# Mamba layer on one core: z*C of two groups in eight is added into a neighbouring group by GpSimd-issued accumulating transfers, and TensorE sums six groups

## What is computed

```python
dA  = exp(einsum('bld,dn->bldn', delta, A))          # 512 channels d, 16 states n
dBx = einsum('bld,bln->bldn', delta * x, Bm)
def step(z, inp):
    dA_t, dBx_t, c_t = inp
    z = dA_t * z + dBx_t
    y = einsum('bdn,bn->bd', z, c_t)                 # the sum over the 16 states
    return (z, y)
y = y + x * D
```

## Time and profile before

| what | us |
|---|---|
| median of 3 runs | 3613.94 |
| lowest, highest | 3609.24, 3613.96 |
| the profiled execution's own time | 3609.97 |
| its span, first to last instruction | 3608.1 |
| of it, Mamba phase, about | 50 to 1680 |
| of it, attention phase, about | 1680 to 3608 |

### The profile page before, as it was taken

The page is one execution under the profiler, slowest core; times in us unless marked ns, Lnnn a source line. Parts: engine busy times, 40 slices in busy tenths (PEclk is TensorE's granted clock), DMA queues, the critical chain, the costliest instruction groups (busy, mean ns, idle before and its releaser), DMA issues.

```text
span 3608.1 us, 119462 instructions
## 1 busy us (share of the span) xinstructions
PE 3386.7 (94%) x51938; PEld 1549.7 (43%) x51938; DVE 3122.9 (87%) x3007; ACT 2536.4 (70%) x3847; POOL 1740.1 (48%) x1559
## 2 busy tenths in 40 slices
PE   7999999999999999997899999999999999999997
PEld 4556555555555555554323323233232332332322
DVE  6898888889898888986897997989979989799896
ACT  4666657676666757664398695985958959679598
POOL 5798888879788888975210312203112131121210
PEclk8999999999999999999999999999999999999999
DMA  4544545444544545542702506106052070330700
GB/s 126 140 121 118 142 110 149 124 137 126 141 133 115 147 115 137 138 131 83 119 14 34 85 2 92 28 19 100 2 78 41 3 109 10 60 59 2 106 2 13
DMA packets 145230, 307.74 MB, mean 85 GB/s; under 512 B 24484, under 2 KB 64068, under 8 KB 144452
## 3 DMA queue, kind: packets, MB, share of 16 engines
q1 hardware_dynamic: 144708, 300.10, 36.3%
HBM read 230.68 MB, written 35.13 MB: 74 GB/s over the span
## 4 chain that ended last, share of the span: by engine, by line
PE 18%; ACT 12%; issue 11%; DVE 10%; DMA 1%; SPq 0%; ACTq 0%; DVEq 0%; POOL 0%
ACT probs L1544 12%; PE ps L1331 6%; PE ps L1316 4%; DVE neg_max L1658 2%; PE ps L1433 2%; PE ps L1366 2%; PE ps L1346 1%; PE ps L1378 1%; PE ps L1277 1%; DVE acc L1815 1%; DVE att L1717 1%; DVE acc L1803 1%; DVE x1T L1640 1%; DVE acc L1748 1%; DVE x1T L1638 1%
## 5 line engine op out<-in xcount | busy, mean ns | idle before, releaser
L353 POOL TENSOR_TENSOR z<-z,c_rep 128x1024 f32<-128x1024 f32 x512 | 1369.5, 2686 | 279.5 <-DVE z L878 270.7
L1544 ACT ACTIVATE probs<-ps,e_scale 128x512 f32<-128x512 f32 x2048 | 1242.4, 702 | 116.4 <-PE ps L1316 114.1
L878 DVE TENSOR_TENSOR_SCAN z<-dA,ps 128x1024 f32<-128x1024 f32 x512 | 1158.8, 2279 | 164.8 <-PE ps L411 114.9
L1658 DVE TENSOR_REDUCE neg_max<-ps 128x1 f32<-128x1024 f32 x1024 | 1187.8, 1217 | 43.9 <-PE ps L1277 42.3
L725 ACT ACTIVATE dA<-rep,a_rep 128x1024 f32<-128x1024 f32 x512 | 566.3, 1142 | 227.6 <-DVE z L878 217.3
L411 PEld LDWEIGHTS ps<-diag,u_t 64*64 64x64 f32 x32768 | 530.6, 136 | 382.7 <-issue 382.4
L1316 PE MATMUL ps<-q_st,k_st 50*128 50x512 f16 x2048 | 632.4, 384 | 35.4 <-ACT probs L1544 28.6
L411 PE MATMUL ps<-diag,u_t 64*64 64x64 f32 x32768 | 596.8, 222 | 54.8 <-DVE z L878 35.8
L1331 PE MATMUL ps<-probs,v_h 128*32 128x256 f32 x8192 | 647.7, 390 | 0.6 <-ACT o_sb L1551 0.6
L1277 PE MATMUL ps<-k_st,q_st 48*128 48x512 f16 x2048 | 600.1, 384 | 7.1 <-DVE neg_max L1658 6.2
L433 PE MATMUL ps<-z,eye 128*64 128x512 f32 x2048 | 503.7, 611 | 21.8 <-ACT ps L653 19.9
(11 more groups left out here) (184 smaller groups left out, 2808.3 us busy)
## 6 DMA issues: line engine op xcount, KB each, us to landing
c_rep<-c_scratch SPq DMA_DIRECT2D x512, 256.0 KB, 4.0
rep<-delta SPq DMA_DIRECT2D x128, 256.0 KB, 5.5
q_st<-qk_halves SPq DMA_DIRECT2D x192, 128.0 KB, 9.9
k_st<-qk_halves SPq DMA_DIRECT2D x192, 128.0 KB, 10.6
qk_halves<-qk_parts SPq DMA_DIRECT2D x32, 512.0 KB, 10.8
x_nat<-in_x SPq DMA_DIRECT2D x9, 1024.0 KB, 7.8
x_rows<-x_nat SPq DMA_DIRECT2D x9, 1024.0 KB, 7.4
xT<-in_xT SPq DMA_DIRECT2D x8, 1024.0 KB, 7.9
```

The costliest lines, as they stand in the source:

```text
L353: pool.tensor_tensor(z[:, k % ZR, :], z[:, k % ZR, :], c_rep[:, slot, :], ALU.mult).then_inc(s_zc, 1)
L878: dve.tensor_tensor_scan(z[:, k % ZR, :], dA[:, k % AR, :], pair(1 + k % 2), 0.0, ALU.mult, ALU.add).then_inc(s_z, 1)
L1544: act.activation(probs[:, kt, half * HALF:(half + 1) * HALF], ps[:, ring_bank(("probs", h, 2 * kt + half)), :], ACT.Exp, scale=e_scale[:, ...
L1658: dve.tensor_reduce(neg_max[:, h % 2, qt:qt + 1], pair(qt % 2), AX.X, ALU.max, negate=True).then_inc(s_mx, 1)
```

## The change

In each slice, groups 1 and 4 (`JOINED`) are no longer added by TensorE. After the second product of the next group (2 or 5), GpSimd waits for its own product, and from the second transfer on for the transfer before, and issues one transfer that adds the two slots of the joined group to the two slots of the next group, in SBUF (`accum_op=ALU.add`). It moves 2 slots x 4 KB x 128 partitions = 1024 KB from and to the tile `z`. TensorE's add of group 2 or 5 waits for the transfer's semaphore `s_acc` and counts two on `s_y`. Where a scan is to reuse the slots of a joined group, VectorE waits on `s_acc` in place of `s_y`. There are 2 joins in a slice, 8 in a block, 64 in all.

```diff
--- before.py
+++ after.py
@@ -189,6 +189,7 @@
         s_zc = sem("zC_ready")
         s_y = sem("zC_added")
         s_seed = sem("sums_seeded")
+        s_acc = sem("z_joined")
         s_yg = sem("y_gated")
         s_o = sem("out_proj_done")
         s_r = sem("residual_added")
@@ -204,6 +205,12 @@
 
         U = M * NG * QN
         CONSTS = 5
+        JOINED = (1, 4)
+        JOINS = len(JOINED)
+
+        def joins(block, n):
+            return 16 * (block * JOINS + n + 1)
+
         WEIGHTS = 16 * (3 + 2 + 1 + QS * QN + 1 + M)
         RAW = 2
         X_ORDER = (0, 2, 3, 1)
@@ -343,6 +350,14 @@
                         if j < KC - 1:
                             pool.wait_ge(s_cvp, 2 * j)
 
+            def join(i, n):
+
+                to, of = (i - 1) % ZR, (i - 3) % ZR
+                pool.wait_ge(s_zc, i + (1 + CZ))
+                if n:
+                    pool.wait_ge(s_acc, n * 16)
+                pool.dma_start(z[:, to:to + 2, :], z[:, of:of + 2, :], accum_op=ALU.add).then_inc(s_acc, 16)
+
             def units(b):
                 for k in range(U):
                     i = b * U + k
@@ -351,6 +366,9 @@
                     if k % QN == 0:
                         pool.wait_ge(s_cr[slot], b * (GR // CR * QS * 16) + (k // QN // CR + 1) * (QS * 16))
                     pool.tensor_tensor(z[:, k % ZR, :], z[:, k % ZR, :], c_rep[:, slot, :], ALU.mult).then_inc(s_zc, 1)
+                    m, g, j = k // 16, k // QN % NG, k % QN
+                    if g - 1 in JOINED and j == 1:
+                        join(i, (b * M + m) * JOINS + JOINED.index(g - 1))
 
             first_conv()
             for b in range(NB):
@@ -427,13 +445,17 @@
                 m, g = grp // NG, grp % NG
                 if g == 0:
                     start_sums(b, m)
+                if g in JOINED:
+                    return
                 pe.wait_ge(s_zc, b * U + (grp * QN + QN + CZ))
+                if g - 1 in JOINED:
+                    pe.wait_ge(s_acc, joins(b * M + m, JOINED.index(g - 1)))
                 for half in range(2):
                     for j in range(QN):
                         mm = pe.matmul(ps[j * QD:(j + 1) * QD, half, :], eye[:, :],
                                        z[:, (grp * QN + j) % ZR, half * HALF:(half + 1) * HALF],
                                        start=False, stop=(g == NG - 1), skip_group_check=True)
-                mm.then_inc(s_y, 1)
+                mm.then_inc(s_y, 2 if g - 1 in JOINED else 1)
 
             def out_proj(b, t):
 
@@ -871,7 +893,10 @@
                 c = b + 1
                 for k in range(U):
                     i = b * U + k
-                    if k % QN == 0:
+                    back = b * GR + k // QN - ZR // QN
+                    if k % QN == 0 and back >= 0 and back % NG in JOINED:
+                        dve.wait_ge(s_acc, joins(back // NG, JOINED.index(back % NG)))
+                    elif k % QN == 0:
                         dve.wait_ge(s_y, b * GR + (k // QN + 1))
                     dve.wait_ge(s_dbx, i + 2)
                     dve.wait_ge(s_da, i + (AR + 1))
```

## The result

The changed kernel takes 3904.1 us (median of 4, 3900.0 to 3911.9) against 3614.0: ratio 1.081, 95% interval 1.079 to 1.083. It is 290 us slower where I had forecast 101 us, and 4 us above the upper end of my range. The sign and the place were right, the size was not.

A forecast was written before the change was run, and what follows sets the result against it. TensorE was taken as the fullest engine, in a loop of scan, dBx and scan. Per block, 14.5 us late less 1.4 gained gave 13.1, 105 us in 8 blocks; 3610 + 105 = 3715 us, range 3585 to 3900.

The forecast's parts named there:

- The sign: Whole kernel: slower than before, chance 0.76; faster 0.19, about unchanged 0.05.
- the place: Mamba phase: TensorE's waiting adds wait for the transfer, 80 to 130 us in all, longest at each block's third and fourth join.
- The bound: Mamba phase: TensorE fullest, busy 1556 of 1630 us, its time worth something only where others wait for it.
- The room rule: At each join, product-to-landing time above the room (5.28 to 10.83 us) moves the scan and all behind by the difference.
- The sum: Eight joins of a block: 14.5 us late, 1.4 gained at the second, net 13.1 us a block, 105 in 8.
- the shortest way from the start of the add to that scan is 3.15 us: Joins: least time from TensorE's waiting add through dBx to VectorE's scan, used to work out how late a landing may be.
- L: Each join: time from the end of GpSimd's product to the transfer's landing, taken as 9.4 us, bounded by 5.8 and 13.4.
- Traffic: DMA engines: share up from 0.47 to about 0.77; 0 to 2 us a block for rep loads, in the range only.
- GpSimd's issue: GpSimd's queue: 0.3 to 3 us per transfer, costed at nothing, hidden by the 29.5 us GpSimd waits in a block.

## Why the prediction was wrong

**The bound, the place and the sign** held. TensorE's time was worth half of its length (61 of 124 us), more than I had named: without transfers the second join's place gives 2.0 us a block and the fifth's 1.6, and the rest of the 61 us came at places that I had counted as worth nothing (all by the scans' starts in both traces, mean over six blocks).

**The room rule** held in form. A join whose add starts later than its room delays its scan by the difference, and by what the way behind the add is longer; the ones with the least room lose most: over the blocks the third and fourth join (slice 1) lose 7.9 and 7.3 us, the fifth 0.7 together with its gain. I had reckoned the third and fourth at 4.1 and 3.3. The run with the plain copy and the one with split transfers move in the direction that it gives.

**The sum, with what was measured.** From the product to the scan, the eight joins of a block take 35.2 us more than before, and the block is 35.8 us longer (both averaged over blocks two to seven): what was lost, was lost on the path that the sum is about. Of the 35.2 us, 22.4 are adds that start later than the room, and 12.8 are what the ways behind the adds have over 3.15 us each. The sum had 13.1 and nothing. Over eight blocks that is 74 us and 102 us too little; 3610 + 105 + 74 + 102 is 3891, of 3904 measured.

**The step that failed** is the term "the shortest way from the start of the add to that scan is 3.15 us". I took it from rows in which TensorE had been busy, and left it as it was behind a wait. Behind its waits for the transfer TensorE runs at the lower clock at most places, and there the way is 5.1 us on average and 5.65 in the rows above; over all eight joins it is 4.75, which makes the 102 us. That the clock does it is shown by the idle work in the wait: it brought the way back to 3.15 us where it lasted long enough, and where it was fitted it made the kernel 33 us faster.

**L** is the second term that was too small. The landing itself was forecast well, 9.6 us against 9.4. But the sum let the add start at the landing, and there are 0.9 us between the last packet and the first matmul: 10.6 us from product to waiting add. With 10.6 for L the sum gives 22.7 us a block in place of 13.1. That the landing came out so near is in part luck: the copy was 7.6 and not 5.8 us, and the accumulation added 2.0 and not 3.8. On the second, the Trainium skill, "Collectives: The Full Stack", section "The bandwidth ceiling", says of reducing transfers in collectives that the two source reads halve the rate; here a packet takes 1.7 times as long as a plain one, so the trace agrees roughly. On the first, the fit in the Trainium skill, "DMA: Bandwidth & Descriptors", section "Anatomy of one DMA", gives an estimate of 4.4 us, far under the 7.6 us of the plain copy in this traffic.

**Traffic.** I had raised the share of the DMA engines to 0.77 and costed 0 to 2 us a block for the loads of rep. The share is 0.56, and ScalarE waits 3.6 us a block longer for rep. In the changed kernel all stretches outside the eight ways from product to scan grew by 0.6 us a block together, so little of it shows there; what it costs inside them the runs don't part. The idle transfers alone cost 5 us a block. With SP as the issuer, 41 us over, the pauses of TensorE inside dBx grow by 27 us, on an engine that I had not looked at for this; with GpSimd as the issuer, 44 us over, they grow by 12 us only, and the scans moved by VectorE's collisions come on top.

**GpSimd's issue**, costed at nothing with 0.3 to 3 us for its length, is 0.88 us, and its own length doesn't show. What I missed is that it shifts the products against VectorE's two-input operations, which grow by some 80 us in the changed kernel. There they fall between a product and a scan that waits for TensorE longer still: behind the make_u of 4.89 us VectorE stood idle for another 4.08 us, as the scan at 1115.11 shows. With the idle transfers from GpSimd, where no add waited for a transfer, two of them in a block were exposed.

## What to carry to other kernels

A wait put into an engine's queue has a room, which can be read off ahead of time, place by place: what is late at each is what it costs, so put transfers only where the room is larger than a measured landing and the start of the work behind it. Price the work behind a wait by rows at the low clock, and see whether the way from the wait to the next engine was read at the high one. Look at what an added instruction shifts: GpSimd's issue of 0.88 us moved its products onto VectorE's operations. And look for added traffic in every engine's waits, TensorE's unexplained pauses among them.

## What the runs showed of the hardware

- An accumulating transfer from SBUF to SBUF takes 0.66 us per packet of 8 KB, a copy 0.39; 1024 KB land 9.6 us after the product that they follow, 7.6 as a copy. An add that waits for them starts 0.9 us later still. Issuing one takes GpSimd 0.88 us, as a copy 0.59.
- After standing still for 5.6 us TensorE worked at a granted clock of 0.60 over the next six microseconds; idle matmuls in the wait kept it up (adds of 1.94 us again in place of 3.68), and fitted to each wait they made the kernel 33 us faster.
- TensorE paused in the middle of groups of matmuls, up to 1.8 us in the kernel before, up to 3.0 with 64 more transfers of 1024 KB from SP and up to 4.8 with 128, mostly until 1.3 to 1.6 us after a packet of 16 KB of the instruction queue had landed.
- A VectorE operation with both inputs in SBUF that starts while GpSimd's product is running waits for it, and for the next product too where that follows at once: make_u took 4.89 us from 1106.14 us on in the changed kernel, while three products ran one behind the other from 1102.70 to 1109.93. In the kernel before it took 1.20 us in the median and 1.58 at most.
